# AdaLN transformer layer with attention and routed experts on one Trainium2 core: the routing part in another order, norm refinement on GpSimd, the last attention step turned in one go

## What is computed

```python
h = layernorm(x) * (1 + ca) + sa
x = x + ga * attention(h)          # 16 heads of 128, causal
h = layernorm(x) * (1 + cb) + sb
x = x + gb * ffn(h)

def ffn(x):                        # x: 2048 x 512
    scores = softmax(x @ gate_weight.T)                 # 8 experts
    topk_w, topk_idx = top_k(scores, 2)
    topk_w = topk_w / (sum(topk_w) + 1e-20)
    y = sum over e of cw[:, e] * (silu(x @ w_gate[e].T) * (x @ w_up[e].T)) @ w_down[e].T
    return y + shared_mlp(x)       # F = 352 per expert, shared width 704 = two more experts
```

## Time and profile before

| | us |
|---|---|
| median of three runs | 1694.1 |
| the profiled execution, its time | 1690.27 |
| the profiled execution, span from first to last instruction | 1688.4 |
| TensorE busy with matmuls | 1590.7 |
| VectorE busy | 898.1 |
| ScalarE busy | 697.6 |
| GpSimd busy | 602.6 |

### The profile page before, as it was taken

One profiled execution on the slowest core, in us unless ns is written; L12 is line 12 of the kernel. 1 busy time (PEld: TensorE's weight loads), 2 busy tenths in 40 slices (PEclk: granted clock), 3 DMA queues, 4 the chain that ended last, 5 costly groups with the idle time before them and its releaser, 6 DMA issues.

```text
span 1688.4 us, 29975 instructions
## 1 busy us (share of the span) xinstructions
PE 1590.7 (94%) x9012; PEld 1379.2 (82%) x9013; DVE 898.1 (53%) x2102; ACT 697.6 (41%) x1689; POOL 602.6 (36%) x641
## 2 busy tenths in 40 slices
PE   6999989999999999999999999868998799999997
PEld 3888578888888888888888888767887688888896
DVE  4323136666656566666666565877565322222267
ACT  4222155555555555555555555431231123232232
POOL 0001034554554535545445445744215111111143
PEclk9999999999999999999999999998998999999998
DMA  7522225243343344342524334584212344665555
GB/s 262 197 109 103 88 71 162 80 126 107 98 136 87 94 129 123 100 124 62 161 84 125 108 91 120 182 289 174 62 56 107 148 176 178 219 228 195 180 184 179
DMA packets 178453, 232.42 MB, mean 138 GB/s; under 512 B 78600, under 2 KB 137352, under 8 KB 175328
## 3 DMA queue, kind: packets, MB, share of 16 engines
q1 hardware_dynamic: 168112, 204.76, 37.1%
q0 software_dynamic: 5680, 18.62, 3.8%
q10 hardware_dynamic: 4608, 8.39, 1.5%
HBM read 151.72 MB, written 80.00 MB: 137 GB/s over the span
## 4 chain that ended last, share of the span: by engine, by line
PE 76%; DVE 9%; DMA 7%; ACT 3%; issue 3%; POOL 1%; SPq 1%; POOLq 0%; ACTq 0%; DVEq 0%
PE bank L1117 45%; PE bank L1194 9%; PE bank L1275 7%; PE bank L1229 7%; DMA slot_results<-y_sb 6%; PE bank L1258 4%; PE bank L1130 1%; PE bank L1326 1%; PE bank L1352 1%; DVE o_lo L1595 1%; DVE pt_lo L1593 1%; ACT o_hi L971 1%; DVE h L1760 1%; POOL tile_hot L799 1%; DVE ht_lo L1778 1%
## 5 line engine op out<-in xcount | busy, mean ns | idle before, releaser
L1117 PE MATMUL bank<-w,xt_hi 128*128 (+2 forms) x1136 | 286.4, 334 | 17.7 <-issue 8.0
L938 ACT ACTIVATE prob<-bank,neg_max 128x128 f32<-128x128 f32 (+3 forms) x256 | 134.2, 526 | 237.9 <-DVE neg_max L1634 235.4
L1117 PEld LDWEIGHTS bank<-w,xt_hi 128*128 128x128 f32 x1136 | 198.8, 192 | 30.7 <-issue 26.2
L679 POOL CAST q_hi<-q_raw 128x512 fp32r<-128x512 f32 x64 | 71.0, 1109 | 383.9 <-PE bank L1229 235.4
L1117 PE MATMUL bank<-w,xt_lo 128*128 (+2 forms) x568 | 185.9, 327 | 0.0
L1117 PE MATMUL bank<-w,ht_hi 128*128 (+3 forms) x426 | 143.1, 417 | 22.2 <-DVE ht_lo L1778 22.1
L1778 DVE TENSOR_TENSOR ht_lo<-bank,ht_hi 128x128 fp32r<-128x128 f32 (+1 forms) x213 | 48.4, 282 | 213.9 <-ACT ht_hi L1051 213.8
L1117 PE MATMUL bank<-wv_hi,h_lo 128*128 128x256 f32 x512 | 144.6, 282 | 0.0
L1117 PE MATMUL bank<-wv_lo,h_hi 128*128 128x256 f32 x512 | 144.4, 282 | 0.0
L1117 PE MATMUL bank<-wv_hi,h_hi 128*128 128x256 f32 x512 | 144.2, 282 | 0.0
L950 ACT ACTIVATE prob<-prob,row_inv 128x128 f32<-128x128 f32 (+3 forms) x256 | 136.3, 557 | 1.4
(11 more groups left out here) (192 smaller groups left out, 4045.8 us busy)
## 6 DMA issues: line engine op xcount, KB each, us to landing
ch_raw<-wexp SPq DMA_DIRECT2D x128, 170.0 KB, 2.7
experts_hi<-ch_hi SPq DMA_DIRECT2D x128, 170.0 KB, 2.0
experts_lo<-ch_lo SPq DMA_DIRECT2D x128, 170.0 KB, 2.2
w<-experts_hi SPq DMA_DIRECT2D x10, 2176.0 KB, 8.7
w<-experts_lo SPq DMA_DIRECT2D x10, 2176.0 KB, 15.2
q_transposed<-q_out SPq DMA_DIRECT2D x64, 256.0 KB, 2.0
q_raw<-q_transposed SPq DMA_DIRECT2D x32, 512.0 KB, 4.4
slot_results<-y_sb SPq DMA_DIRECT2D x39, 256.0 KB, 2.0
```

Source lines behind the costliest of these rows:

```text
L679: pool.tensor_copy(hi, raw).then_inc(split_hi, 1)
L938: ins = act.activation(prob[:, h, ROW_AT[r]:ROW_AT[r] + (r + 1) * P], bank[2 + i % 2][:, at:at + (r + 1) * P], ACT.Exp, bias=neg_max[:, h, ...
L1117: ins = pe.matmul(dst, a, m, start=(k == 0), stop=(k == last))
```

## The change

Four parts. (1) `tile_match` goes from GpSimd (32 operations of 128x40) to VectorE (four of 128x640), in front of `lanes(0, 0)` and `lanes(1, 0)`. (2) The tables are no longer products with coefficient rows and sums: one comparison and one sum give the number of experts begun, and shifts and small operations on 39 columns give the rest; all of it is in front of job 21's VectorE work, where it had ended behind. GpSimd's queue: `gather_x(1)`, both `weights_ready(0)` and `(1)` now stand ahead of the adds of jobs 20 and 21, and `gather_x(2)` directly behind them. (3) The four refinement operations of the second norm go from VectorE to GpSimd, behind the seed. (4) In the last attention step TensorE turns head 0 and all of head 1, into banks 2, 3 and 0, before both `weigh`; it waits for the last `pt_lo` before `turn_rows(0)`.

```diff
+def pt_bank(h, g, last):
+    return (2, 3, 0)[g] if last and h == 1 else 4 + g % 2
...
             def c_seed_of(b):
                 pool.wait_ge(c_var, b + 1)
                 pool.tensor_tensor(rs0[:, :], ve[:, :], mh[:, :], ALU.pow).then_inc(c_seed, 1)
+                pool.wait_ge(c_seed, b * C_SEED + 1)
+                pool.tensor_tensor(nt1[:, :], rs0[:, :], rs0[:, :], ALU.mult).then_inc(c_seed, 1)
+                pool.wait_ge(c_seed, b * C_SEED + 2)
+                pool.tensor_tensor(nt2[:, :], nt1[:, :], ve[:, :], ALU.mult).then_inc(c_seed, 1)
+                pool.wait_ge(c_seed, b * C_SEED + 3)
+                pool.tensor_scalar(nt1[:, :], nt2[:, :], -0.5, 1.5, ALU.mult, ALU.add).then_inc(c_seed, 1)
+                pool.wait_ge(c_seed, b * C_SEED + 4)
+                pool.tensor_tensor(rstd[:, :], nt1[:, :], rs0[:, :], ALU.mult).then_inc(c_seed, 1)
...
             gather_x(0)
-            for n in range(NT + 3, R0 - 1):
+            for n in range(NT + 3, R0 - 2):
                 add_shared(n)
             gather_x(1)
             pool.wait_ge(tab_ok, 1)
...
             weights_ready(0)
+            weights_ready(1)
+            add_shared(R0 - 2)
             add_shared(R0 - 1)
-            for r in range(1, NSLOT):
+            gather_x(2)
+            for r in range(2, NSLOT):
                 weights_ready(r)
...
                 turn(0, (0, 1))
+                if last:
+                    turn(0, (2,))
+                    turn(1, (0, 1, 2))
+                    weigh(0)
+                    weigh(1)
+                    return
...
-            pe.wait_ge(s_exp, NIT * 6)
+            pe.wait_ge(pt_ok, NIT * 6)
             turn_rows(0, 0, loaded(0, 0, False))
...
+            def tile_match(c):
+                link(dve.tensor_tensor(tile_eq[:, c, :, :],
+                                       cf("slot_tile", NOH).unsqueeze(1).to_broadcast([P, NT, NOH]),
+                                       pos_f[:, c, 1, :].unsqueeze(2).to_broadcast([P, NT, NOH]), ALU.is_equal))
+                dve.tensor_tensor(tile_hot[:, c, :, :], tile_eq[:, c, :, :],
+                                  cf("token", NT).unsqueeze(2).to_broadcast([P, NT, NOH]),
+                                  ALU.mult).then_inc(tile_hot_ok, 1)
...
+                link(dve.tensor_reduce(j_f[:, 0, 1:], j_le[:, :, :], AX_X, ALU.add))
+                link(dve.tensor_copy(j_u[:, 0, :], j_f[:, 0, 1:]))
+            def halves():
+                link(dve.tensor_scalar(j_u[:, 1, :], j_u[:, 0, :], 1, None, ALU.logical_shift_right))
+                link(dve.tensor_scalar(j_u[:, 2, :], j_u[:, 0, :], 3, None, ALU.logical_shift_right))
+                link(dve.tensor_copy(j_f[:, 1:3, 1:], j_u[:, 1:3, :]))
+            def table():
+                count, odd, all_ = (j_f[:, k, 1:] for k in range(3))
+                link(dve.scalar_tensor_tensor(out=j_f[:, 3, 1:], in0=odd, scalar=-2.0, in1=count,
+                                              op0=ALU.mult, op1=ALU.add))
...
+                dve.tensor_tensor(tab[:, 4, :], j_f[:, 4, 1:], tab[:, 5, :], ALU.subtract).then_inc(tab_ok, 1)
...
+            tile_match(0)
             lanes(0, 0)
             shared_job(NT + 2, lambda: lanes(0, 1))
+            tile_match(1)
             lanes(1, 0)
             shared_job(NT + 3, lambda: lanes(1, 1))
             begun()
-            table(0)
             slot_tokens()
-            shared_job(NT + 4, lambda: table(1))
-            table(2)
-            table(3)
-            shared_job(NT + 5, lambda: table(4))
-            table(5)
-            tables_done()
+            shared_job(NT + 4, halves)
+            table()
+            shared_job(NT + 5)
             weights()
```

More of the change, by code:

```diff
@@ L108, in coefficients @@
         "tiles": np.repeat(j, E),
[L110 to L115, removed]
         "lane": np.arange(P),
@@ L793, in _ @@
             add_shared(NT)
[L795 to L805, removed]
             for n in range(NT + 1, NT + 3):
@@ L963, in pt_part @@
                     act.wait_ge(pt_full, n * 6 + (3 * h + g + 1))
-                    act.activation(pt_hi[:, PT_AT[g]:PT_AT[g] + PT_LEN[g]], bank[4 + g % 2][:, 0:PT_LEN[g]],
+                    act.activation(pt_hi[:, PT_AT[g]:PT_AT[g] + PT_LEN[g]], bank[pt_bank(h, g, last)][:, 0:PT_LEN[g]],
                                    ACT.Copy).then_inc(pt_hi_ok, 1)
@@ L1253, in turn @@
                         blocks = PT_GROUPS[g]
-                        if not (first and h == 0 and g < 2):
+                        if last and h == 1:
+                            if g == 2:
+                                pe.wait_ge(v_ok, n * 2 + 1)
+                        elif not (first and h == 0 and g < 2):
                             pe.wait_ge(pt_ok, n * 6 + (3 * h + (1 if g == 2 else 0)))
@@ L1258, in turn @@
                                 ins = pe.transpose(
-                                    bank[4 + g % 2][:, at + (r - k) * P:at + (r - k + 1) * P],
+                                    bank[pt_bank(h, g, last)][:, at + (r - k) * P:at + (r - k + 1) * P],
                                     prob[:, h, ROW_AT[r] + k * P:ROW_AT[r] + (k + 1) * P], ident[:, :])
@@ L1651, in pt_part @@
                     cols = slice(PT_AT[g], PT_AT[g] + PT_LEN[g])
-                    low(pt_lo[:, cols], bank[4 + g % 2][:, 0:PT_LEN[g]], pt_hi[:, cols], None, pt_ok)
+                    low(pt_lo[:, cols], bank[pt_bank(h, g, last)][:, 0:PT_LEN[g]], pt_hi[:, cols], None, pt_ok)
                 def o_part(h):
@@ L1956, in begun @@
                 first_ = e1[:, 3, :].unsqueeze(1).to_broadcast([P, NSLOT, E])
+                dve.memset(j_f[:, 0, 0:1], 0.0)
                 link(dve.tensor_tensor(j_le[:, :, :], first_, tiles, ALU.is_le))
-                link(dve.tensor_tensor(j_eq[:, :, :], first_, tiles, ALU.is_equal))
-            def table(row):
-                src, name = ((j_le, "parity"), (j_le, "even"), (j_le, "odd"),
-                             (j_le, "next"), (j_eq, "load_0"), (j_eq, "load_1"))[row]
-                weight = cf(name, E).unsqueeze(1).to_broadcast([P, NSLOT, E])
-                link(dve.tensor_tensor(j_t[:, :, :], src[:, :, :], weight, ALU.mult))
-                link(dve.tensor_reduce(j_f[:, row, :], j_t[:, :, :], AX_X, ALU.add))
-            def tables_done():
-                dve.tensor_copy(tab[:, :, :], j_f[:, :, :]).then_inc(tab_ok, 1)
+                link(dve.tensor_reduce(j_f[:, 0, 1:], j_le[:, :, :], AX_X, ALU.add))
[8 more added lines that the diff above has]
+                                              op0=ALU.mult, op1=ALU.add))
+                link(dve.tensor_tensor(j_f[:, 4, 1:], count, j_f[:, 0, 0:NSLOT], ALU.subtract))
+                link(dve.tensor_scalar(tab[:, 0, :], j_f[:, 3, 1:], -1.0, 1.0, ALU.mult, ALU.add))
+                link(dve.tensor_tensor(j_f[:, 5, 1:], count, odd, ALU.subtract))
+                link(dve.tensor_scalar(tab[:, 1, :], j_f[:, 5, 1:], 32.0, None, ALU.mult))
+                link(dve.tensor_scalar(tab[:, 2, :], odd, 1.0, 32.0, ALU.add, ALU.mult))
+                link(dve.tensor_tensor(tab[:, 3, :], count, all_, ALU.add))
+                link(dve.tensor_tensor(tab[:, 5, :], j_f[:, 4, 1:], j_f[:, 3, 1:], ALU.mult))
+                dve.tensor_tensor(tab[:, 4, :], j_f[:, 4, 1:], tab[:, 5, :], ALU.subtract).then_inc(tab_ok, 1)
             shared_job(NT - 4, lambda: less_max(ROUTES[0]))
```

22 lines of the change are left out of this document (6 added, 16 removed).

## The result

| | before | after |
|---|---|---|
| median of four runs each (us) | 1692.66 | 1674.60 |
| lowest and highest | 1689.21, 1695.77 | 1670.39, 1678.04 |
| the profiled execution, its time | 1690.27 | 1676.70 |
| the profiled execution, span | 1688.4 | 1674.9 |

The changed kernel is faster: the ratio of the two is 0.9893, with a 95% interval of 0.9859 to 0.9926. In shares that is 1.07%, 18.1 us of the median; between the two profiled executions it is 13.5 us of span. The forecast was 16 us and 1678 us. One execution of batch 0 on VectorE took 1952.59 us at a granted clock of 0.746 and is left out of that kernel's median and ratio.

The account below looks back on a forecast made before the run. TensorE was taken to bound the kernel, busy 1590.7 of 1688.4 us, so only its waits and low clock could yield gains. Terms 5.6 + 6.7 + 0.3 + 2.7 + 0.8 + 0.2 gave 16.3: 1678 from median 1694.1, range 1668 to 1688.

Parts of the forecast that it names:

- part 1, to `turn_rows(21)`: Around `slot_tokens(0)`: `tile_match` on VectorE removes the 6.0 us gap and job 19 starts sooner, 5.6 us gained.
- part 2, to `turn_rows(26)`: Job 22 to the gather: earlier tables and memsets remove TensorE's waits, a longer gather wait returns some, 6.7 us gained.
- part 3, batch 2, to `turn_rows(8)`: Batch 2's norm rows start sooner on VectorE but are slowed by `c_pre(3)`: the 6.12 us gap becomes 3.4, 2.7 gained.
- part 3, batch 3, to `turn_rows(17)`: Batch 3's norm refinement on GpSimd cuts a TensorE gap from 1.36 us to 0.5, 0.8 gained.
- parts 3 and 4, batches 0 and 1, to `turn_rows(2)`: Batch 0's refinement gains 0.3 us; job 1 starts 0.1 to 0.3 sooner, with the turning's 0.7 loss contained.
- partly at full clock: `slot_tokens(0)` after the gap before `down(17)`: 1.2 GHz lasts 3.9 us, to 1282.5, and it ends at about 1284.6.
- still with a low clock behind it: Batch 2's gap, shrunk from 6.12 to 3.4 us, would still be followed by TensorE at 1.2 GHz.
- rival (b): Shrunken gaps at 1276 and 1162 stay at 2.4 GHz, batch 1's rows meet less `c_pre`: gain 22, 1672 us; chance 0.16.
- Batch 0's term: Batch 0's four refinement operations take 1.3 us on GpSimd against 1.8 on VectorE: 0.3 us gained.
- (a): VectorE-GpSimd locks and small GpSimd operations at upper bounds, gather landing in 10.7 us: gain 9, 1685 us; chance 0.22.
- (c): `weights_ready(1)` blocks the adds, waiting for a second expert's weights; gather 10 us later, gain 6, 1688 us; chance 0.04.
- (d): TensorE stays at 1.2 GHz from 1113 us on through closer gaps; slower kernel, 1698 us with 40 us more; chance 0.03.

Follow-up runs that it names:

- batch 0 on VectorE: Changed kernel with the norm refinement of batch 0 alone put back on VectorE: 1677.24 us (three executions), ratio 0.9889 to the kernel before.
- the second profile: The changed kernel run and profiled again, unedited, on the chip of three later variants: 1675.28 us, ratio 0.9881 to the kernel before.
- tokens late: Changed kernel with `gather_x(2)` ahead of the adds, batch 1's statistics behind head 1's last `pt_lo`, both `slot_tokens` behind job 19: 1667.69 us, ratio 0.9844.
- all moves: As tokens late, plus `gather_x(3)` ahead of job 21's add and batch 1's last two row tiles behind job 0's `xt_lo`: 1661.88 us, ratio 0.9798.
- part 4 alone: Kernel before with only the last attention step's heads both turned before `weigh`: 1696.58 us, ratio 1.0019.

## Why the prediction came out right

The total was right, and two of its terms were off by 1.6 and 2.3 us, in opposite directions.

| term | predicted gain | measured in its stretch |
|---|---|---|
| part 1, to `turn_rows(21)` | 5.6 | 4.0 |
| part 2, to `turn_rows(26)` | 6.7 | 6.9 |
| part 3, batch 2, to `turn_rows(8)` | 2.7 | 5.0 |
| part 3, batch 3, to `turn_rows(17)` | 0.8 | 0.9 |
| parts 3 and 4, batches 0 and 1, to `turn_rows(2)` | 0.5 | 1.2 - 0.8 = 0.4 |
| sum | 16.3 | 17.2 |

The measured sum, 17.2 (16.5 against the second profile), agrees with the 18.1 us of the medians, whose interval is some 5.6 us to either side. The forecast time, 1678, was 3.4 above the median measured: it started from the median of three runs of the kernel before, 1694.1, which with a fourth is 1692.66, and the gain was forecast 2 us smaller than it came out. The profiled pair shows 13.5 because its first stretch is 3.3 us longer after than before and its last 0.6; as the second profile shows, such differences come and go without the code.

**Part 1.** Right: `tile_match` takes 0.83 + 0.82 us (1.7 forecast); `tile_hot` is gone from the waits; `slot_tokens(0)` follows without a gap; the second one costs nothing, though its `tile_hot` took 1.77 us beside a GpSimd add. The step that was mis-sized is "partly at full clock": I allowed some 4 us at 1.2 GHz behind the gap, to 1282.5, and it lasted ten, from about 1276. My own rows should have warned me, as they have the clock at 0.50 for all 8.00 us from 1285 to 1293. The price of `ht_lo` going back was a gap of 3.25 us against 3.7.

**Part 2.** Right in both its halves, and in the one that mattered most: the gather is waited for longer, because it still hangs on the add of job 21. It landed in 8.07 us (8.8 taken) and was waited for 6.2 (6.6). The table ended at 1302.65; it had been forecast for 1310.3 on the time scale of the kernel before, where `turn_rows(21)` stands 7.2 us later: nearly the same place. One small operation was held up for 1.16 us beside GpSimd's add, as forecast. The Trainium skill ("SBUF — State Buffer", Who interferes with whom) has the lock for VectorE instructions with two SBUF inputs, or in a faster mode that this trace doesn't show. The row operations agree, at 1.71 to 1.77 us beside GpSimd's 128x512 operations where they take 0.74 alone; this operation has one input, and whether it ran in that mode no run here shows.

**Part 3.** Right: the rows of batch 2 start sooner and are slowed by `c_pre(3)`. The gap of 6.12 us became 3.0 (3.4 forecast), in part since a refinement operation takes 0.28 us with its wait and not 0.33, 0.2 us in four. The step that failed is "still with a low clock behind it": the first two matmuls took 0.74 and the clock is 1.00 from 1165 to 1175 us, where before it was 0.73. Of ten profiles with this refinement, all with a gap of 2.7 to 3.0 us here, eight have the clock up behind it and two, tokens late and all moves, have it low after all, so this gain isn't sure in every kernel. That was rival (b)'s mechanism, and it decided in this place, while at 1276 the opposite of (b) came in. The two errors, +2.3 and -1.6, nearly cancel; the sum was right partly for that reason, which is luck. Batch 0's term shows as a gap of 1.89 in place of 2.65 us in step 30, 0.76 where 0.3 was taken, in a stretch too unsteady to count it; the measured 0.4 of the table's last term is batch 1 and part 4 alone.

**Part 4.** The predicted gap near 4.6 us is there (4.66), and the first output product comes 0.8 us later (0.7 forecast), though that stretch is less steady than this, and with part 4 alone nothing of the 0.8 was left at `turn_rows(2)`.

**The rivals.** (a) fell: small GpSimd operations stand at 0.20 us, not near 1, and the second `tile_match` found cover. (c) fell: the memset of `weights_ready(1)` was at 1305.43, 1.26 us behind the first, without a wait for weights. (d) fell: TensorE was at 1.2 GHz for some 34 us before and some 31 after between head 0 and `turn_rows(26)`, worked out from the granted clock in windows of some 5 us.

## What to carry to other kernels

When a wait is removed from a queue, look at what the next item in the same queue hangs on: here `gather_x(2)` stood behind an add that needed a job's end, and moving one line brought 7.3 us, as much as part 2 with its new tables and its other moves had brought (6.9). When the start of a stage waits for two engines, only the later one counts: taking 1.9 us off TensorE before job 1 left 0.4 us at most, taking two tiles' rows from VectorE cut the wait from 6.00 to 1.46. Compare two executions by landmarks, stretch by stretch, since two spans of one kernel agreed within 0.5 us while two of its stretches differed by 6 us each way.

## What was unexpected of the hardware

- TensorE's clock behind a gap can't be read off the gap's length. Gaps of 2.96, 3.00 and 2.06 us were followed by two matmuls in 0.72 to 0.74 us, and one of 2.04 us by the same two in 1.22. Behind 3.00 us, with the same code around it, the clock stayed at 1.00 in the changed kernel and fell a microsecond later in tokens late. Behind 3.58 us the 1.2 GHz came at once and lasted some 3 us; behind 3.25 us it came a microsecond later and lasted ten.
- The low level can hold while TensorE has no idle time at all: 10.00 us busy of 10.00 at 0.50. It also came with gaps of only 0.5 and 0.6 us right before it, in tokens late.
- A GpSimd operation on 128x4 takes 0.20 us, and the power on the same shape 1.02.
